# Where the projection and the statistics of the next tile stand in an attention unit

## The chip, the cores and the metric

The kernel runs on one core of a Trainium2 chip. The metric is the device time of the whole kernel in microseconds (us), lower is better. A core has a matmul engine (TensorE, in the profile PE, with its weight loads as PEld), a vector engine (VectorE, DVE), an engine for activation functions (ScalarE, ACT), a general one (GpSimd, POOL), and SyncE (SP), which here only issues DMAs. Each engine works through its own queue in order, and they meet through semaphores.

## What is computed

One layer of a transformer, for x of 8 sequences with 512 tokens of 256 values, in float32: a modulated layer norm, causal attention with 16 heads of 16 values and rotary positions, a gated residual, a second modulated layer norm, and a feed-forward layer with eight experts, of which each token takes one. Cut to what matters:

```python
h = layernorm(x) * (1 + ca) + sa
Q, K, V = h @ Wq.T + bq, h @ Wk.T + bk, h @ Wv.T + bv      # 16 heads of 16
Q, K = rope(Q, pos), rope(K, pos)
scores = where(causal, Q @ K^T / 4, -1e9)
attn = softmax(scores) @ V
x = x + ga * (attn @ Wo.T + bo)
h = layernorm(x) * (1 + cb) + sb
x = x + gb * route_prob_max * expert_of_token(h)            # 8 experts, gelu
```

The change is in the attention part alone, and there in the first three lines of it: the statistics of the layer norm, and the projection to Q and K.

## The kernel before

Tokens are cut into 32 tiles of 128 (four to a sequence), heads into four groups of four. The attention part works in 32 **units** (U = 0 to 31): unit U is one group of heads of one sequence, all 512 queries against all 512 keys. Each engine has its own loop over the units, in an order that is written out by hand: TensorE's at L791, ScalarE's at L954, VectorE's at L1192, GpSimd's at L513, SyncE's at L364.

A unit has six **shots**, s = 0 to 5. In each shot TensorE makes two things:

- the maxima products of the *next* unit V = U + 1 (`max_scores`, L646 and L653): scores in one layout, 768, 768, 1024, 1024, 1024 and 512 columns wide in the six shots, into the two banks `ps_max`. VectorE reduces them to row maxima (`maxima`, L1116). `ps_max` is a single buffer: the products of shot s wait until VectorE has reduced shot s - 1.
- the scores of *this* unit (`scores`, L680) into the two banks `ps_sc`, which ScalarE turns into exponentials (`exps`, L926). `ps_sc` is a single buffer too, and shot s waits for the exponentials of shot s - 1.

Between them the rest of the work is laid in by hand:

- the weighting of the values by the exponentials (`weigh`, L693), of which two parts of unit U - 1 stand in shot 0;
- the work on the tile T = U + 5, five ahead. `project_qk` (L599 to L607) projects its 128 tokens to 256 values of Q and 256 of K in the bank `ps_b`: a bias matmul (L604), then one float32 matmul of 512 columns for each of the KC = 2 halves of the 256 inputs (L605); each such matmul has two records in the profile. VectorE's `rope` (L1087, L1093) reads `ps_b`, GpSimd's `rotate` (L425) adds the two products, ScalarE (L890) and VectorE (`lo_parts`, L1102, L1103) split the sum into 16-bit parts, and TensorE transposes these in shot 5;
- the statistics of tile T + 1 on VectorE (`statistics`, L1063, L1065, L1067), GpSimd's power of its variance (`rstd_of`, L417), VectorE's `normalise` (L1072) in shot 4, TensorE's transposes of it (L596) at the end of the unit, and VectorE's `modulate` (L1079), whose result the next `project_qk` multiplies;
- the output projection and the residual of older units, and, once in four units (U = 11, 15, 19, 23, 27), the logits of the router for four tiles (`logit_products`, L739).

At the end of the unit VectorE negates the maxima (`negated`, L1123), TensorE transposes them with the queries (`shift_rows`, L663), and ScalarE keeps these (L919) for the next unit's scores. VectorE's `rope` follows `maxima(V, 1)`, and its `statistics` follow `maxima(V, 2)`.

Tiles 0 to 4 are projected before the units, in a lead phase, where both halves and the values' projection (L613) follow each other with nothing between. Units from 27 on have no tile to project; units from 26 on have no statistics to take. The experts' part comes behind the attention part, from about 530 us on.

Of the kernel before, what the change touches and what calls it, by code (L numbers as in the profile page):

```python
# [19 lines left out]
NT = B * QT  # L20
KC = D // P
# [45 lines left out]
def ge(eng, sem, count):  # L67

    if isinstance(count, int) and count <= 0:
        return  # L70
    eng.wait_ge(sem, count)
# [43 lines left out]
def attention_part(nc, sem, x, wq, bq, wk, bk, wv, bv, wo, bo, c, wmod, rope_cos, rope_sin, switch_w, switch_b,  # L115
                   w1, w2, row_dram, mods_dram, w_dram, logits, ident, sw_b):
    with ExitStack() as ctx:
# [3 lines left out]
        def bank(name):  # L121
            return ctx.enter_context(nc.psum_tensor(name, [P, 512], F32))
# [54 lines left out]
        ps_a, ps_b = bank("ps_a"), bank("ps_b")  # L177
# [369 lines left out]
        def _(pe):  # L547
# [51 lines left out]
            def project_qk(T, k, ps, kept_before):  # L599

                if k == 0:
                    pe.wait_ge(ht_done, KC * T + KC)
                    ge(pe, qt_kept, kept_before)
                    mm(ps, ones3[:, :], bias3[:, 0:2 * D], start=True, stop=False)  # L604
                last = mm(ps, h_t[:, k, :], w_qkv[:, k, 0:2 * D], start=False, stop=(k == KC - 1))  # L605
                if k == KC - 1:
                    last.then_inc(qk_ps, 1)  # L607
# [77 lines left out]
            def weigh(U, kb):  # L685
                par, g = place(U)
                pe.wait_ge(masked, QT * U + kb + 1)
                L = S - P * kb
                p_kb = prob[:, U % 2, P_AT[kb]:P_AT[kb + 1]].rearrange("p (j m q) -> p j m q", j=2, m=2)
                for m in range(2):  # L690
                    for j in range(2):
                        col = 2 * m + j
                        last = mm(ps_pv[32 * col:32 * col + 32, kb * P:S], v_sb[:, par, kb, HG * g + col, :],  # L693
                                  p_kb[:, j, m, :], start=(kb == 0), stop=(kb == QT - 1), skip_group_check=True)
                if kb == 0:
                    last.then_inc(pv0_ps, 1)
                if kb == QT - 1:
                    last.then_inc(pv_ps, 1)
# [92 lines left out]
            for U in range(NU):  # L791
                T, V, X, Z = U + LEAD, U + 1, U - QT, U - LAG
                for s in range(NSHOT):
                    if V < NU:
                        max_scores(V, s)
                    scores(U, s)
                    if s == 0 and U:
                        weigh(U - 1, 2)
                        weigh(U - 1, 3)
                    if s == 1 and Z > 0 and Z % QT == 0:  # L800
                        pe.wait_ge(x1_done, X)
                        logit_products(Z // QT - 1, ps_nd)
                    if s < KC and T < NT:
                        project_qk(T, s, ps_b[:, :], T)
                    if s == 1 and Z > 0 and Z % QT == 0:
                        logit_transposes(Z // QT - 1, ps_nd)
                    if Z >= 0 and s == h_shot(Z):
                        ge(pe, logits_kept, Z // QT)
                        pe.wait_ge(x1_done, X)
                        h_transposes(Z, ps_nd)  # L810
                    if s == 2:
                        if T < NT:
                            project_v(T, ps_a[:, :], T)
                        ge(pe, htr_kept, Z + 1)
                        if U:
                            tokens_first(U - 1)
                    if s == 3:
                        if U == 0:
                            pe.wait_ge(mods_kept, 1)
                        weigh(U, 0)  # L820
                    if s == 4:
                        if X >= 0:
                            pe.wait_ge(att_done, U)
                            ge(pe, x1_done, X)
                            att_transposes(X, ps_nd)
                        weigh(U, 1)
                    if s == 5:
                        if X >= 0:
                            project_out(X, ps_nd)
                        if T < NT:  # L830
                            q_transposes(T, ps_b[:, :])
                        if V < NU:
                            shift_rows(V)
                        if T < NT:
                            k_transposes(T, ps_a[:, :])
                        if T + 1 < NT:
                            if U == 0:
                                pe.wait_ge(gates_kept, 1)
                            x_transposes(T + 1, ps_nd, U)
# [171 lines left out]
        def _(dve):  # L1011
# [48 lines left out]
            def statistics(T):  # L1060
                par, t = place(T)
                dve.wait_ge(xs_loaded[loaded_by(T)], tile_loads(T))
                nc.vector.bn_stats(bn[:, :], xs[:, par, t, :]).then_inc(stats_done, 1)  # L1063
                dve.wait_ge(stats_done, T + 1)
                nc.vector.bn_aggr(mean_var[:, :], bn[:, :]).then_inc(mv_done, 1)  # L1065
                dve.wait_ge(mv_done, T + 1)
                nc.vector.tensor_scalar(var_eps[:, :], mean_var[:, 1:2], LN_EPS, None, ALU.add).then_inc(var_done, 1)  # L1067
# [68 lines left out]
            def residual(X, ps):  # L1136
                par, t = place(X)
                dve.wait_ge(xr_loaded[loaded_by(X)], tile_loads(X))
                dve.wait_ge(const_added, X + 1)
                dve.wait_ge(o_ps, X + 1)  # L1140
                x1 = rows[:, par, t, D:2 * D]
                nc.vector.tensor_tensor(x1, ps[:, KC * P:KC * P + D], x1, ALU.add).then_inc(x1_done, 1)
# [49 lines left out]
            for U in range(NU):  # L1192
                T, V, X = U + LEAD, U + 1, U - QT
                for s in range(NSHOT):
                    if V < NU:
                        maxima(V, s)
                    if s == 0 and X > 0:
                        residual(X - 1, ps_nd)
                    if s == 1 and T < NT:
                        rope(T, ps_b[:, :])  # L1200
                    if s == 2 and T + 1 < NT:
                        statistics(T + 1)
                    if s == 3 and U:
                        divide(U - 1)
                    if s == 4:
                        if T < NT:
                            lo_parts(T)
                        if T + 1 < NT:
                            normalise(T + 1)
                if V < NU:  # L1210
                    negated(V)
                if T < NT:
                    keep_qt(T, ps_b[:, :])
                if X > 0:
                    row_statistics(X - 1)
                if T + 1 < NT:
                    modulate(T + 1, ps_nd)
# [509 lines left out]
```

## Time and profile before

| | us |
|---|---|
| median of 3 runs | 790.11 |
| lowest and highest | 788.54, 791.86 |
| the profiled execution's own time | 788.82 |
| span of its instructions | 787.0 |
| busy in it: PE, DVE, ACT, POOL | 698.1, 597.4, 506.4, 455.0 |
| mean granted clock of PE | 0.967 of full |

The profile shows one execution. A row of a timeline gives the start of an instruction and its length in us, the engine, the line of the kernel, what it writes and reads, and how many neighbouring instructions are merged in the row; in brackets stands for how long the engine was idle before it, and which instruction of another engine ended that. Matmuls are pipelined, and their ends are modelled, so that one can begin before the one before it has ended; the distance from start to start is the safer measure. "PEclk" is the clock that TensorE was granted, as a part of full speed, or in tenths of it.

### The profile page before, as it was taken

The numbers are of one execution on the slowest core, as the hardware profiler recorded it, in microseconds if no ns is written. First come the engines' busy times: TensorE is split into PE (matmuls) and PEld (weight loads), VectorE is DVE, ScalarE is ACT, GpSimd is POOL, SyncE is SP. The second block draws the span as 40 slices with busy tenths as digits, with TensorE's granted clock in tenths as the row PEclk, the third lists the DMA queues.
The fourth block names the chain that finished last, engine by engine and source line by source line (L and its number), as shares of the span: only waits on it lengthen the run. The fifth ranks groups of instructions, "written<-read, shape, count | busy, mean of one in ns | idle before, by whom it ended". The sixth has DMA issues, their size and how long they took to land. (4 is left out here: it accounts for less than half of the span.)

```text
span 787.0 us, 20856 instructions
## 1 busy us (share of the span) xinstructions
PE 698.1 (89%) x7310; PEld 433.4 (55%) x7310; DVE 597.4 (76%) x1238; ACT 506.4 (64%) x1001; POOL 455.0 (58%) x577
## 2 busy tenths in 40 slices
PE   6858889999999999999999888755999999999993
PEld 4533434455455544554554443434788878788772
DVE  5767787988988978879889767348577777777774
ACT  1426788888888888888888878733444444444441
POOL 4313454777777777777777868851254444445331
PEclk8998999999999999999999999966999999999998
DMA  8104233244344443534633537539666642232100
GB/s 266 41 1 102 89 92 110 69 128 132 115 149 122 137 133 110 148 121 95 152 104 113 154 101 163 133 109 384 223 205 213 212 139 78 82 89 85 35 20 0
DMA packets 61362, 97.48 MB, mean 124 GB/s; under 512 B 8404, under 2 KB 42317, under 8 KB 60752
## 3 DMA queue, kind: packets, MB, share of 16 engines
q1 hardware_dynamic: 56272, 79.36, 34.0%
q0 software_dynamic: 4992, 16.79, 6.8%
q8 instruction: 64, 1.05, 0.5%
q14 instruction: 34, 0.28, 0.1%
HBM read 69.47 MB, written 34.51 MB: 132 GB/s over the span
## 5 line engine op out<-in xcount | busy, mean ns | idle before, releaser
L1116 DVE TENSOR_REDUCE row_max<-ps_max 128x2 f32<-128x768 f32 (+2 forms) x192 | 199.6, 1040 | 51.2 <-PE ps_max L653 51.1
L926 ACT ACTIVATE prob<-ps_sc 128x1024 f32<-128x1024 f32 (+1 forms) x192 | 169.2, 882 | 60.4 <-PE ps_sc L680 59.4
L1464 PE MATMUL ps_h<-tok_t,w_all 128*128 128x128 f16 x1872 | 156.4, 219 | 0.6 <-DVE tok_t L1639 0.3
L1464 PEld LDWEIGHTS ps_h<-tok_t,w_all 128*128 x1872 | 130.8, 98 | 41.8 <-issue 2.1
L1534 ACT ACTIVATE hid<-ps_h,b_t 128x128 f32<-128x128 f32 x312 | 89.3, 368 | 95.3 <-PE ps_h L1464 95.3
L434 POOL TENSOR_SCALAR_AFFINE_SELECT prob<-prob 128x512 f32<-128x512 f32 x128 | 82.5, 645 | 86.5 <-ACT prob L926 86.1
L1381 POOL DMA_INDIRECT slot_mem<-row_dram,token x39 | 55.7, 1428 | 120.3 <-DVE y L1674 99.8
L1477 PE MATMUL ps_y<-w_all,hid_parts 128*128 x312 | 118.0, 379 | 1.3 <-DVE hid_parts L1649 1.3
L693 PE MATMUL ps_pv<-prob,v_sb 128*32 128x512 f32 (+3 forms) x1024 | 88.8, 442 | 0.3 <-POOL prob L434 0.2
L646 PE MATMUL ps_max<-k_t,q_t 64*128 64x512 f16 (+3 forms) x512 | 68.6, 304 | 22.8 <-DVE row_max L1116 22.1
L1479 PE MATMUL ps_y<-w_all,hid_parts 128*128 x312 | 85.1, 273 | 0.0
L646 PEld LDWEIGHTS ps_max<-k_t,q_t 64*128 64x128 f16 x512 | 20.3, 93 | 117.2 <-DVE row_max L1116 64.6
L482 POOL TENSOR_TENSOR halves<-raw,halves 128x512 f16<-128x512 f32 x64 | 74.3, 1161 | 17.0 <-ACT raw L936 17.0
L680 PE MATMUL ps_sc<-q_t,k_t 64*128 64x256 f16 (+3 forms) x512 | 67.4, 300 | 5.2 <-ACT q_t L919 4.8
L1647 DVE CAST hid_parts<-hid 128x512 f16<-128x512 f32 x78 | 33.8, 433 | 48.3 <-ACT hid L1534 48.3
L605 PE MATMUL ps_b<-w_qkv,h_t 128*128 128x512 f32 x120 | 70.3, 674 | 0.0
L1398 POOL DMA_INDIRECT out<-y,token x39 | 43.0, 1104 | 29.7 <-DVE y L1674 19.6
L425 POOL TENSOR_TENSOR rot<-rot_a,rot_b 128x512 f32<-128x512 f32 x32 | 40.7, 1271 | 29.2 <-DVE rot_b L1093 28.7
L1649 DVE TENSOR_TENSOR hid_parts<-hid,hid_parts 128x512 f16<-128x512 f32 x78 | 54.2, 694 | 2.7
L653 PE MATMUL ps_max<-tri,tri_w 64*128 64x64 bf16 (+1 forms) x768 | 46.5, 199 | 0.0
L919 ACT ACTIVATE q_t<-ps_sc 128x512 f16<-128x512 f16 x64 | 34.7, 593 | 17.9 <-PE ps_sc L663 17.4
L653 PEld LDWEIGHTS ps_max<-tri,tri_w 64*128 64x128 bf16 x768 | 36.9, 95 | 12.4 <-issue 0.3
(257 smaller groups left out, 1322.3 us busy)
## 6 DMA issues: line engine op xcount, KB each, us to landing
raw<-w SPq DMA_DIRECT2D x64, 256.0 KB, 3.0
w_dram<-halves SPq DMA_DIRECT2D x64, 256.0 KB, 3.3
w_all<-w_dram SPq DMA_DIRECT2D x20, 512.0 KB, 4.6
row_dram<-rows SPq DMA_DIRECT2D x32, 256.0 KB, 3.4
w_all<-w_dram SPq DMA_DIRECT2D x3, 2048.0 KB, 13.0
mod_rows<-mods_dram SPq DMA_DIRECT2D x16, 256.0 KB, 7.2
row_dram<-mods_dram SPq DMA_DIRECT2D x32, 128.0 KB, 4.4
xs<-x SPq DMA_DIRECT2D x24, 128.0 KB, 3.3
```

What stands on the lines that cost most here:

```text
L434: nc.gpsimd.affine_select(out=diag, in_=diag, compare_op=ALU.is_ge, fill=0.0, base=0, pattern=[[0, HG], [1, P]], channel_multiplier=-1).th ...
L482: nc.gpsimd.tensor_tensor(lo, piece_raw(m)[0], hi, ALU.subtract).then_inc(w_lo[m % 2], 1)
L605: last = mm(ps, h_t[:, k, :], w_qkv[:, k, 0:2 * D], start=False, stop=(k == KC - 1))
L646: mm(ps_max[:, j, m * L:(m + 1) * L], q_t[rows, par, pair, qt * P:(qt + 1) * P], k_t[rows, par, pair, 0:L], start=(m == 0), stop=False, sk ...
L653: last = mm(o, tri_w[rows, side, :], tri[rows, 0:n, :], start=False, stop=(side == 1), skip_group_check=True)
L693: last = mm(ps_pv[32 * col:32 * col + 32, kb * P:S], v_sb[:, par, kb, HG * g + col, :], p_kb[:, j, m, :], start=(kb == 0), stop=(kb == QT ...
L926: nc.scalar.activation(p_kb[:, :, first * L:(first + n) * L], ps_sc[:, :, 0:n * L], ACT.Exp, scale=SCALE).then_inc(exp_done, 1)
L1116: nc.vector.tensor_reduce(dst, ps_max[:, :, 0:n * L].rearrange("p j (m l) -> p j m l", m=n), AX.X, ALU.max).then_inc(max_done, 1)
L1464: last = mm(o, w[:, :, k, f, :][:, bass.ds(e, 1), :].rearrange("p e m -> p (e m)"), tok_t[:, j % 2, piece, k, :], start=(n == 0 and f % HF ...
L1477: mm(ps_y[j % 2][:, :], hid_hi[:, j % 2, f, :], w2_both[:, :, f, :, :][:, bass.ds(e, 1), :, :].rearrange("p e a d -> p (e a d)"), start=(f ...
L1479: last = mm(ps_y[j % 2][:, 0:D], hid_lo[:, j % 2, f, :], w2_both[:, :, f, 0, :][:, bass.ds(e, 1), :].rearrange("p e d -> p (e d)"), start= ...
L1534: ins = nc.scalar.activation(hid[:, j % 2, f, :], ps_h[j % 2][q][:, (f % HF) * P:(f % HF + 1) * P], ACT.Gelu_apprx_tanh, bias=b1_t[:, bass ...
```

## The change

In each unit TensorE gives up the first half of the projection of queries and keys in shot 0 (bias matmul and one float32 matmul, behind the weighting), and makes bias matmul and both halves together in shot 1, behind the second maxima products and the second scores. In VectorE's queue the three instructions of the statistics move from behind the third maxima (shot 2) to between the second maxima (shot 1) and the rope. Nothing is added or removed, and what is computed stays the same.

```diff
@@ TensorE, in the loop over the units @@
                     if s == 1 and Z > 0 and Z % QT == 0:
                         pe.wait_ge(x1_done, X)
                         logit_products(Z // QT - 1, ps_nd)
-                    if s < KC and T < NT:
-                        project_qk(T, s, ps_b[:, :], T)
+                    if s == 1 and T < NT:
+                        for k in range(KC):
+                            project_qk(T, k, ps_b[:, :], T)
                     if s == 1 and Z > 0 and Z % QT == 0:
                         logit_transposes(Z // QT - 1, ps_nd)
@@ VectorE, in the loop over the units @@
                         maxima(V, s)
                     if s == 0 and X > 0:
                         residual(X - 1, ps_nd)
+                    if s == 1 and T + 1 < NT:
+                        statistics(T + 1)
                     if s == 1 and T < NT:
                         rope(T, ps_b[:, :])
-                    if s == 2 and T + 1 < NT:
-                        statistics(T + 1)
                     if s == 3 and U:
                         divide(U - 1)
```

## Rows read from the trace of the kernel before

**Rows 1.** The page, sections 1 and 2: busy time, and the clock in 40 slices.
```profile
PE 698.1 (89%) x7310; PEld 433.4 (55%) x7310; DVE 597.4 (76%) x1238; ACT 506.4 (64%) x1001; POOL 455.0 (58%) x577
...
PEclk8998999999999999999999999966999999999998
```

**Rows 2.** The waits: who waited for whom, us in all, times, the longest.
```profile
DVE rot_a L1087 <- PE ps_b L605: 16.8, 30, 3.2
```

**Rows 3.** Timeline of VectorE, a steady unit: start, length, engine, line, output and input.
```profile
309.49 0.69 DVE L1087 TENSOR_TENSOR rot_a<-ps_b,cos_t 128x512 f32<-128x512 f32 x1 [0.31 <-PE ps_b L605]
...
310.76 1.21 DVE L1116 TENSOR_REDUCE row_max<-ps_max 128x4 f32<-128x1024 f32 x1
311.89 0.42 DVE L1063 BATCH_NORM_STATS2 bn<-xs 128x6 f32<-128x256 f32 x1
...
312.56 0.15 DVE L1067 TENSOR_SCALAR var_eps<-mean_var 128x1 f32<-128x1 f32 x1
312.63 1.22 DVE L1116 TENSOR_REDUCE row_max<-ps_max 128x2 f32<-128x1024 f32 x1
...
317.68 0.20 DVE L1123 TENSOR_SCALAR q_aug<-row_max 128x16 f16<-128x16 f32 x1
...
323.70 0.69 DVE L1087 TENSOR_TENSOR rot_a<-ps_b,cos_t 128x512 f32<-128x512 f32 x1 [0.31 <-PE ps_b L605]
```

**Rows 4.** Timeline of TensorE, the same unit and the one after.
```profile
306.42 0.38 PE L604 MATMUL ps_b<-bias,ones 3*128 3x512 bf16 x1
306.73 1.13 PE L605 MATMUL ps_b<-w_qkv,h_t 128*128 128x512 f32 x2
307.79 0.34 PE L646 MATMUL ps_max<-k_t,q_t 64*128 64x384 f16 x2
...
308.02 0.38 PE L680 MATMUL ps_sc<-q_t,k_t 64*128 64x512 f16 x2
308.33 1.13 PE L605 MATMUL ps_b<-w_qkv,h_t 128*128 128x512 f32 x2
309.29 0.38 PE L731 MATMUL ps_nd<-ident,rows 128*128 128x128 f32 x2
...
317.94 0.62 PE L663 MATMUL ps_sc<-ident,q_aug 128*128 128x128 f16 x8 [0.25 <-DVE q_aug L1123]
```

**Rows 5.** Timeline, the first shot of that unit on VectorE and ScalarE.
```profile
305.71 0.95 DVE L1116 TENSOR_REDUCE row_max<-ps_max 128x2 f32<-128x768 f32 x1
305.74 1.02 ACT L926 ACTIVATE prob<-ps_sc 128x1024 f32<-128x1024 f32 x1 [0.49 <-PE ps_sc L680]
```

**Rows 6.** Timelines, products that wait for a reduction, and reductions that wait for products.
```profile
69.75 1.22 DVE L1116 TENSOR_REDUCE row_max<-ps_max 128x2 f32<-128x1024 f32 x1
...
71.51 1.23 DVE L1116 TENSOR_REDUCE row_max<-ps_max 128x2 f32<-128x1024 f32 x1 [0.55 <-PE ps_max L653]
...
312.03 0.39 PE L646 MATMUL ps_max<-k_t,q_t 64*128 64x512 f16 x2 [0.26 <-DVE row_max L1116]
...
312.32 0.33 PE L680 MATMUL ps_sc<-q_t,k_t 64*128 64x384 f16 x2
```

**Rows 7.** Timeline of TensorE in the lead phase, a projection in one piece.
```profile
28.89 1.98 PE L605 MATMUL ps_b<-w_qkv,h_t 128*128 128x512 f32 x4
30.71 1.03 PE L613 MATMUL ps_a<-w_qkv,h_t 128*128 128x256 f32 x4
```

**Rows 8.** Timeline, the first two shots of unit 0.
```profile
62.62 0.94 DVE L1116 TENSOR_REDUCE row_max<-ps_max 128x2 f32<-128x768 f32 x1
...
63.63 0.50 PE L646 MATMUL ps_max<-k_t,q_t 64*128 64x384 f16 x2
...
64.59 1.98 PE L605 MATMUL ps_b<-w_qkv,h_t 128*128 128x512 f32 x2
...
66.61 0.69 DVE L1087 TENSOR_TENSOR rot_a<-ps_b,cos_t 128x512 f32<-128x512 f32 x1 [1.38 <-PE ps_b L605]
```

**Rows 9.** Stretches: busy PE, PEld, DVE, ACT, POOL, then PEclk, DMA share, GB/s.
```profile
66.00:67.00 1.00, 1.00 (x11) 0.36 (x10) 0.39 (x1) 0.00 (x0) 0.45 (x1) 0.82 0.36 87
```

## The prediction

> **What bounds the kernel now.** I read the page first for the shares of the engines [rows 1]: TensorE is busy for 89% of the span and its clock is granted in full in nearly every slice of the attention part. High shares of two engines say little about which wait ends last, so I went on to the list of waits [rows 2]: VectorE's first rope product waited 30 times for the projection of queries and keys, 16.8 us in all. Then I laid the timelines of VectorE and TensorE of one steady unit beside each other, and followed them round.
>
> From the rope at 309.49 to the end of the negated maxima at 317.68 + 0.20 = 317.88, VectorE has no gap [rows 3]. The shift transposes of TensorE start at 317.94, right behind it [rows 4], and from there TensorE has no gap until the last pass of the next projection; the rope of the next unit starts at 323.70, 14.21 us after the last one [rows 3]. So the loop has two legs: a VectorE leg of 8.4 us, from rope to negated maxima, and a TensorE leg of 5.8 us, from shift transposes to the end of the projection. Both edits lie on it. The projection closes the TensorE leg; the statistics stand in the VectorE leg. 27 units project (units 0 to 26), 26 take statistics (0 to 25). Whatever one edit adds to a steady unit is paid some 26 times.
>
> **First part: both halves of the projection behind the second scores.** Before, the stretch in question is this [rows 4]: bias matmul at 306.42, first half at 306.73 (0.31 later), second maxima products at 307.79 (1.06), second scores at 308.02 (0.23), second half at 308.33 (0.31), and the rope at 309.49 (1.16) [rows 3]. Together 3.07 us from the bias matmul to the rope.
>
> The first half now fills a time in which TensorE would have to wait: both maxima banks form one buffer, and the second maxima products may start only when VectorE has reduced the first. That reduction runs from 305.71 to 306.66 [rows 5]. With the half gone from there, TensorE is through with the weighting at 306.42 and waits at the second maxima products; queued behind that wait are the second scores, the whole projection and the transposes of h. The hand-over from reduction to products takes 0.06 us elsewhere (311.97 to 312.03) [rows 3, 6], so the products start at 306.72. The scores follow 0.29 later, as they do behind another such wait (312.03 to 312.32) [rows 6]; they also need the first exponentials, which end at 305.74 + 1.02 = 306.76 [rows 5], before 307.01, so that doesn't bind. The bias matmul follows 0.31 behind the scores (as 308.02 to 308.33), the first half 0.31 behind the bias [rows 4].
>
> For the fused projection the lead phase has the very sequence. There the four records of a projection take 1.98 us, and the next instruction starts 1.82 us after the first [rows 7]. Split, the two pairs are followed by their next instruction after 1.06 and, where that is again a float32 operation, 0.96 (308.33 to 309.29) [rows 4]: 2.02. Fusing saves 0.20 us of TensorE, at one change from 16-bit to float32 work and back. The rope starts 0.03 behind the last record (308.33 + 1.13 to 309.49), so 2.01 from the first half to the rope.
>
> New stretch from the end of the reduction at 306.66: 0.06 + 0.29 + 0.31 + 0.31 + 2.01 = 2.98 us, against 309.49 - 306.66 = 2.83 before. **The rope comes 0.15 us later** in each of units 1 to 26: +3.9 us. The lower end takes the bias matmul 0.23 behind the scores instead of 0.31 (nearest row: 307.79 to 308.02), +0.07 per unit. The upper end denies the saving: 1.06 + 1.16 instead of 2.01, +0.36 per unit.
>
> The Trainium skill, page "TensorE: Matmul & The Clock Gate", section "Back-to-back issue gap", gives an isolated matmul's spacing as its columns over 2.4 GHz plus 2.5 ns, with no term for what its neighbours are. Worked out from it as an estimate, a half costs the same wherever it stands, and fusing saves nothing; the rows of the lead phase speak against that [rows 4, 7]. It is the second rival's side, whose price I take from rows.
>
> Four units (11, 15, 19, 23) have logit products, float32, ahead of the projection. There the bias matmul stands between two float32 pieces and adds one more change of type, 0.10 by half of the 0.20 above: +0.4 us in all, ends 0 and 0.8.
>
> **Unit 0** has no weighting, and its first maxima on VectorE end only at 62.62 + 0.94 = 63.56; the products start at 63.63 [rows 8]. Bias and first half stood wholly under that wait. Now they follow it. TensorE is at half its clock there (1.2 GHz), until about 66.36, by a granted mean of 0.82 in the microsecond from 66 [rows 9]. From products to rope takes 0.29 + 0.31 + 0.31 + 2.01 = 2.92 us at full clock. The 2.73 us up to 66.36 do half of that length's work, 1.37; the remaining 1.55 put the rope at 67.91, against 66.61 [rows 8]: +1.3 us. If the clock stays low throughout, 63.63 + 5.84 = 69.47: +2.9 us. TensorE will stand idle for some 2.4 us before, where it was busy, which makes a later rise possible. I take +1.5, nearer the lower end, because TensorE is busy without a gap from 63.63 on in either order.
>
> The Trainium skill, same page, section "What's actually happening", says that the throttled state is the default and activity lifts it; by that the idle time could only delay the rise, which is the +2.9 end.
>
> **Second part: statistics ahead of the rope.** Three VectorE instructions, 311.89 to 312.56 + 0.15 = 312.71, 0.82 us, leave the gapless leg [rows 3]. But little of it comes back. The third maxima's reduction ends at 310.76 + 1.21 = 311.97, and the fourth starts at 312.63, 0.66 later [rows 3]. Without anything between them VectorE would wait for the refill of the bank: in unit 0, where nothing is done between the fourth and fifth maxima, the distance is 71.51 - (69.75 + 1.22) = 0.54, with a wait for the products noted [rows 6]. **The gain is 0.66 - 0.54 = 0.12 us** per unit, 26 times: -3.1 us. Ends: 0 (the 0.66 stays) and 0.82 (all of it, if the refill were hidden).
>
> In their new place the statistics are covered. The second reduction starts about 0.60 behind its products (as 312.03 to 312.63) [rows 3, 6], at 307.32 at the latest, takes 0.96 and ends at 308.28; the statistics end at 309.10, and the rope is due at 309.64. Cover of 0.54 us; if it were gone, each microsecond of delay would be one of the path. Their wait for the tile of x costs nothing: it is loaded seven units ahead by the loop of SyncE. GpSimd's power of the variance still stands behind the rotation, which waits for the rope; it only finds its input earlier. No DMA moves. ScalarE gets the second scores earlier, but keys and the weighted sum are copied in its queue ahead of them.
>
> **The sum**: 3.9 - 3.1 + 1.5 + 0.4 = +2.7 us. The profiled execution has a span of 787.0 us in 788.82 us; it would become 791.5. The median of three runs is 790.11, 1.3 above the profiled one; on it I predict **792.8 us**.
>
> **The rivals.** A measurement of this kernel can't tell less than about 0.5%, 4.0 us, from no change.
>
> (A) *Forecast*: a wait takes the place of the filler, mostly repaid by fusing and by the statistics. Its own range is 790 to 796. Chance 0.60.
>
> (B) *Slower, no saving from fusing*: in the unit, weights or the change of type cost as much as before, 26 x 0.21 = 5.5 us more, 798.3 us. Place: from bias matmul to rope. It decides the sign once a steady unit is over (4.0 - 1.9) / 26 = 0.08 us longer than 14.21. For it: split passes are slower [rows 4]. Against: four passes in a row are measured at 1.98 [rows 7]. Chance 0.15.
>
> (C) *Slower, no gain from the statistics*: the refill takes 0.66 whatever stands there. 3.9 + 1.5 + 0.4 = +5.8, 795.9 us. Against: 0.54 in unit 0 [rows 6]. Chance 0.08.
>
> (D) *Small gain, the first wait is not felt*: the second products start at 306.42 and the rope keeps its place or comes earlier; then -3.1 + 1.5 = -1.6, 788.5 us. Against: one maxima buffer, and VectorE's reduction held until 306.66 by its own queue [rows 5]. Chance 0.13.
>
> (E) *The edit does what it seems to say*: the leg of VectorE gets 0.82 shorter. 26 x (0.15 - 0.82) + 1.9 = -15.5, 774.6 us. Against: the refill of 0.54 [rows 6]. Chance 0.04.
>
> **How the numbers follow.** The likeliest case gives 792.8. The range 788 to 798 takes in A, C and D and stops just short of B; outside lie B's upper half, E and a tail of A, some 2 in 10. Faster by over 0.5%: E, and 0.03 of D with unit 0 at its cheap end: 0.07. Slower by over 0.5%: B 0.15, C 0.05, and 0.08 of A, where unit 0 costs 2.9 and a unit some 0.1: 0.28. Within: 0.65.
>
> **What would show it.** Rope to rope in steady units: 14.24 says A, 14.45 B, 14.36 C, 14.09 D, 13.5 E. The idle time before the second maxima products should appear as a new wait of TensorE for VectorE's first reduction, about 0.3 us, some 26 times; the wait of the rope in the list should change little in place but shrink or grow with what the statistics fill. Four float32 passes within 1.98 us confirm the saving. Third to fourth reduction: 0.54 instead of 0.66. Rope of unit 0: at about 68. The prediction is wrong at its root if the loop is no longer closed by TensorE's projection, or if the clock falls inside the attention units.

## The result, and the profile of the changed kernel

The changed kernel takes 793.33 us (median of 13 runs, 791.60 to 796.87), the kernel before, in as many runs beside it, 789.72. The ratio is 1.0041, with a 95% interval from 1.0022 to 1.0060: some 3 us slower, 0.4%. The prediction was 792.8 us, within 788 to 798. The profiled execution has a span of 792.5 us in 794.36 us. (The kernel before ran again beside each later run; its medians there are 789.83 to 790.87 us, and each ratio below is to the executions beside it.)

Page of the changed kernel, sections 1 and 2, and two rows of its list of waits; they answer to [rows 1, 2].

```profile
PE 700.2 (88%) x7310; PEld 439.3 (55%) x7310; DVE 598.8 (76%) x1238; ACT 503.5 (64%) x1001; POOL 455.6 (57%) x577
...
PEclk8997999999999999999999989966799999999997
```
```profile
DVE rot_a L1088 <- PE ps_b L605: 30.9, 30, 3.6
...
PE ps_max L646 <- DVE row_max L1117: 29.2, 92, 2.3
```

The shares tell nothing. The waits do: TensorE waits for VectorE's reductions 92 times, 29.2 us (66 times, 22.1 us before), the wait that was forecast. The rope's own wait for the projection was to change little and grew from 16.8 to 30.9 us. That is no loss: VectorE is through with the work ahead of the rope sooner, and stands idle for 0.74 us where it was 0.31. Timeline of VectorE in a steady unit, to be read beside [rows 3]:

```profile
311.65 0.69 DVE L1088 TENSOR_TENSOR rot_a<-ps_b,cos_t 128x512 f32<-128x512 f32 x1 [0.74 <-PE ps_b L605]
...
312.92 1.21 DVE L1117 TENSOR_REDUCE row_max<-ps_max 128x4 f32<-128x1024 f32 x1
314.68 1.23 DVE L1117 TENSOR_REDUCE row_max<-ps_max 128x2 f32<-128x1024 f32 x1 [0.55 <-PE ps_max L653]
...
317.93 0.42 DVE L1104 TENSOR_TENSOR k_aug<-rot,k_aug 128x256 f16<-128x256 f32 x1
318.26 0.72 DVE L1073 TENSOR_SCALAR xhat<-xs,mean_var,rstd 128x256 f32<-128x256 f32 x1
...
319.62 0.21 DVE L1124 TENSOR_SCALAR q_aug<-row_max 128x16 f16<-128x16 f32 x1
...
325.74 0.69 DVE L1088 TENSOR_TENSOR rot_a<-ps_b,cos_t 128x512 f32<-128x512 f32 x1 [0.75 <-PE ps_b L605]
```

From rope to rope it is now **14.09 us, not 14.21**: the steady unit has become faster. The legs, parted here at the start of the negated maxima (the prediction's 8.4 and 5.8 are parted at their end), are 319.62 - 311.65 = 7.97 on VectorE (8.19 before) and 325.74 - 319.62 = 6.12 on TensorE (6.02 before). Timelines of TensorE, first the end of the first reduction on VectorE, to be read beside [rows 4, 5]:

```profile
307.77 0.94 DVE L1117 TENSOR_REDUCE row_max<-ps_max 128x2 f32<-128x768 f32 x1
308.77 0.34 PE L646 MATMUL ps_max<-k_t,q_t 64*128 64x384 f16 x2 [0.24 <-DVE row_max L1117]
...
309.00 0.38 PE L680 MATMUL ps_sc<-q_t,k_t 64*128 64x512 f16 x2
...
309.31 0.39 PE L604 MATMUL ps_b<-bias,ones 3*128 3x512 bf16 x1
...
309.63 1.98 PE L605 MATMUL ps_b<-w_qkv,h_t 128*128 128x512 f32 x4
```

The reduction ends at 308.71; products after 0.06, scores after 0.23, bias after 0.31, projection after 0.32, rope after 2.02: 2.94 us, where 2.98 was forecast and 2.83 was the time before. The loss is elsewhere: above all in unit 0, to be read beside [rows 8, 9].

```profile
63.71 0.50 PE L646 MATMUL ps_max<-k_t,q_t 64*128 64x384 f16 x2 [2.33 <-DVE row_max L1117]
...
65.21 3.78 PE L605 MATMUL ps_b<-w_qkv,h_t 128*128 128x512 f32 x4
...
69.03 0.69 DVE L1088 TENSOR_TENSOR rot_a<-ps_b,cos_t 128x512 f32<-128x512 f32 x1 [2.98 <-PE ps_b L605]
```
```profile
66.00:69.00 3.00, 3.00 (x6) 0.75 (x6) 0.05 (x1) 0.00 (x0) 0.53 (x1) 0.50 0.35 87
...
455.00:460.00 5.00, 4.44 (x26) 1.54 (x22) 3.00 (x4) 3.04 (x5) 1.50 (x4) 0.51 0.00 1
```

Four records take 3.78 us, at half the clock throughout, and the rope comes at 69.03. The second window shows another stretch at 1.2 GHz, from 455 to 462 us, inside the attention units, among those that no longer project.

The table has, for every kernel of this study, the time from the last rope of the lead phase to the rope of unit 0; the part of it from the start of unit 0's first reduction on; a steady unit; and the time from that last lead rope to the rope of unit 26, all from one trace each; then the medians. The time to unit 26 ends before the later clock changes. But the time to unit 0 holds one that isn't the order's: in "statistics only", "halves apart" and "every fourth unit old" TensorE was at half its clock for 6.8 us shortly behind the last lead rope (from 46.5, 47.1 and 47.7 us on), and the first reduction of unit 0 came 22.34 to 22.65 us behind that rope instead of 20.10; in "unit 0 old, warm" for 3.4 us (from 46.4), and it came after 21.10. The column "from its first reduction" leaves that out.

| kernel | to unit 0 | from its first reduction | steady unit | to unit 26 | median us | ratio to before, 95% interval |
|---|---|---|---|---|---|---|
| before | 24.09 | 3.99 | 14.21 | 396.09 | 789.72 | |
| changed | 26.42 | 6.32 | 14.09 | 398.04 | 793.33 | 1.0041 (1.0022 to 1.0060) |
| projection only | 26.43 | 6.32 | 14.31 | 402.39 | 798.70 | 1.0088 (1.0055 to 1.0121) |
| statistics only | 25.99 | 3.49 | 14.33 | 400.73 | 795.38 | 1.0051 (1.0029 to 1.0073) |
| unit 0 as before | 23.95 | 3.85 | 14.09 | 395.62 | 790.37 | 1.0003 (0.9981 to 1.0025) |
| halves apart | 28.67 | 6.33 | 14.40 | 408.24 | 800.78 | 1.0118 (1.0086 to 1.0149) |
| filled wait | 23.98 | 3.87 | 14.09 | 395.54 | 792.47 | 1.0019 (0.9997 to 1.0042) |
| late mask | 24.06 | 3.95 | 14.24 | 396.73 | 793.40 | 1.0031 (1.0011 to 1.0051) |
| more statistics | 26.76 | 6.31 | 14.09 | 398.33 | 794.49 | 1.0051 (1.0026 to 1.0075) |
| every fourth unit old | 26.11 | 3.46 | 14.09, 14.26, 14.31 | 397.82 | 791.91 | 1.0009 (0.9985 to 1.0034) |
| later mask | 24.47 | 4.09 | 14.09 | 394.09 | 790.07 | 0.9990 (0.9974 to 1.0005) |
| before, warm | 24.17 | 4.07 | 14.21 | 396.52 | 789.80 | 0.9994 (0.9977 to 1.0010) |
| unit 0 old, warm | 25.18 | 4.08 | 14.09 | 396.81 | 789.07 | 0.9979 (0.9963 to 0.9994) |
| combined | 22.80 | 2.70 | 14.09 | 392.39 | 786.54 | 0.9950 (0.9930 to 0.9970) |

### The profile page after: what moved, and what is told of

It reads as the page before. It is cut to its first block and busy times, and to the rows that moved or that the text cites. A ratio compares the mean times of both kernels' runs of the same rounds, so it can differ in the third digit from the quotient of the medians.

```text
span 792.5 us, 20856 instructions
## 1 busy us (share of the span) xinstructions
PE 700.2 (88%) x7310; PEld 439.3 (55%) x7310; DVE 598.8 (76%) x1238; ACT 503.5 (64%) x1001; POOL 455.6 (57%) x577
## 5 line engine op out<-in xcount | busy, mean ns | idle before, releaser
L434 POOL TENSOR_SCALAR_AFFINE_SELECT prob<-prob 128x512 f32<-128x512 f32 x128 | 86.9, 679 | 91.3 <-ACT prob L927 88.6
L646 PE MATMUL ps_max<-k_t,q_t 64*128 64x512 f16 (+3 forms) x512 | 69.2, 307 | 29.9 <-DVE row_max L1117 29.2
L605 PE MATMUL ps_b<-w_qkv,h_t 128*128 128x512 f32 x120 | 63.1, 650 | 0.0
```

Source lines behind the costliest of these rows:

```text
L434: nc.gpsimd.affine_select(out=diag, in_=diag, compare_op=ALU.is_ge, fill=0.0, base=0, pattern=[[0, HG], [1, P]], channel_multiplier=-1).th ...
L646: mm(ps_max[:, j, m * L:(m + 1) * L], q_t[rows, par, pair, qt * P:(qt + 1) * P], k_t[rows, par, pair, 0:L], start=(m == 0), stop=False, sk ...
```

## The experiments

**The two parts apart.** The first run leaves the statistics in shot 2:

```diff
-                    if s < KC and T < NT:
-                        project_qk(T, s, ps_b[:, :], T)
+                    if s == 1 and T < NT:
+                        for k in range(KC):
+                            project_qk(T, k, ps_b[:, :], T)
```

> The first part of the change alone: the whole projection behind the second scores, the statistics where they were. In the steady units of the changed kernel the rope comes 2.94 us behind the end of the first reduction instead of 2.83, so this part alone should cost 0.11 us per steady unit, some 0.35 in the four units behind the logit products, and 2.3 us in unit 0. Theory (each part has its own price, and they add up): rope to rope 14.32 us in a steady unit, 795 to 797 us in all. Rival (the part costs nothing per unit and the whole loss is unit 0): 14.21, 792.5 us.

The second moves the statistics alone:

```diff
+                    if s == 1 and T + 1 < NT:
+                        statistics(T + 1)
                     if s == 1 and T < NT:
                         rope(T, ps_b[:, :])
-                    if s == 2 and T + 1 < NT:
-                        statistics(T + 1)
```

> The second part of the change alone: statistics between second maxima and rope, the projection in two halves as before. Theory: they have cover in their new place only because the fused projection starts VectorE's second reduction 1.4 us earlier. Without it the reduction ends at 309.19 in the unit shown and the rope was due at 309.49, so statistics of 0.82 us push the rope by about 0.5 us, of which 0.12 come back at the fourth reduction: 14.6 us from rope to rope, about 799 to 800 us in all. Rival (the statistics are worth their 0.12 us wherever they stand ahead of the rope): 14.09, 787 us.

Measured: 14.31 and 14.33 us. Timelines of VectorE, first of the projection alone:

```profile
315.34 0.69 DVE L1088 TENSOR_TENSOR rot_a<-ps_b,cos_t 128x512 f32<-128x512 f32 x1 [1.48 <-PE ps_b L605]
...
321.71 0.85 DVE L1104 TENSOR_TENSOR k_aug<-rot,k_aug 128x256 f16<-128x256 f32 x1
...
323.53 0.21 DVE L1124 TENSOR_SCALAR q_aug<-row_max 128x16 f16<-128x16 f32 x1
...
329.65 0.69 DVE L1088 TENSOR_TENSOR rot_a<-ps_b,cos_t 128x512 f32<-128x512 f32 x1 [1.48 <-PE ps_b L605]
```

and of the statistics alone:

```profile
312.46 0.41 DVE L1063 BATCH_NORM_STATS2 bn<-xs 128x6 f32<-128x256 f32 x1
...
313.12 0.15 DVE L1067 TENSOR_SCALAR var_eps<-mean_var 128x1 f32<-128x1 f32 x1
313.20 0.68 DVE L1087 TENSOR_TENSOR rot_a<-ps_b,cos_t 128x512 f32<-128x512 f32 x1
...
321.15 0.21 DVE L1123 TENSOR_SCALAR q_aug<-row_max 128x16 f16<-128x16 f32 x1
```

The projection alone lengthens TensorE's leg to 6.12 and leaves VectorE's at 8.19; VectorE then idles 1.48 us ahead of the rope. The statistics alone shorten VectorE's leg to 7.95, but the rope (the next one starts at 327.53) stands behind them without a gap, so the other leg grows to 327.53 - 321.15 = 6.38. That is +0.36, where 0.5 was expected, and VectorE's leg lost 0.24, where 0.12 was expected: 14.33 instead of 14.6. The size of my expectation was off, its sign right. **Each part alone costs, 0.88% and 0.51%, and together they cost no more than either.** The traces say it more sharply than the medians. From the rope of unit 0 to that of unit 26, the projection alone costs 3.96 us and the statistics alone 2.74; together they win 0.38 (375.96, 374.74 and 371.62 against 372.00). Up to unit 26, with unit 0 in it, it is +6.3, +4.6 and +1.95; but of the +4.6, 2.4 are the low clock behind the lead phase that the table names, which the place of the statistics doesn't explain. The idle time that one part opens is the room that the other needs.

**Unit 0.**

```diff
-                    if s == 1 and T < NT:
+                    if s < KC and T < NT and U == 0:
+                        project_qk(T, s, ps_b[:, :], T)
+                    if s == 1 and T < NT and U:
                         for k in range(KC):
                             project_qk(T, k, ps_b[:, :], T)
```

> The changed kernel, but in unit 0 the first half of the projection stays in the first shot, as before. Theory: unit 0 costs 2.3 us by itself, since there the half stood wholly under a wait and TensorE is at half its clock; so the rope of unit 0 is back at 66.6 and the kernel at about 791.0, 0.2% above the kernel before. Rival (the loss is spread over the other units, or a slower clock later in the run costs it): less than 1 us is won, 792.5 or more.

Measured: 23.95 us to unit 0, units at 14.09, 790.37 us, ratio 1.0003. With one unit of 27 in the old order the measurable loss is gone. Up to unit 26 the trace is 2.4 us shorter (395.62 against 398.04), the medians 3.0; the rival's "less than 1 us" fits neither.

```diff
+                    if s == 0 and U == 0:
+                        ge(pe, qt_kept, T)
+                        for _ in range(20):
+                            mm(ps_b[:, 0:P], ident16[:, :], ident16[:, :], start=True, stop=True)
```

> The changed kernel with 20 small matmuls without use laid into the wait of unit 0 (into the bank of the projection, whose first real product overwrites them), so that TensorE is busy there. The order of the real work stays that of the changed kernel. Theory: of the 2.4 us that unit 0 costs, about 1.3 are the order itself, and about 1.1 the clock, which rises some 3 us later because TensorE stood idle for 2.3 us; with the wait filled, last lead rope to rope of unit 0 takes 25.4 us instead of 26.4, and the kernel about 792.2. Rival (the clock rises late for another reason, such as where the execution happens to stand): 26.4 us stays.

Measured: 23.98 us, not 25.4. Timeline of TensorE and VectorE, and the stretches with the granted clock (the last number but two):

```profile
60.71 1.84 PE L800 MATMUL ps_b<-ident 128*128 128x128 f16 x20
...
63.91 1.98 PE L605 MATMUL ps_b<-w_qkv,h_t 128*128 128x512 f32 x4
...
65.93 0.69 DVE L1092 TENSOR_TENSOR rot_a<-ps_b,cos_t 128x512 f32<-128x512 f32 x1 [0.74 <-PE ps_b L605]
```
```profile
60.00:62.00 2.00, 1.83 (x16) 1.40 (x17) 1.90 (x4) 1.14 (x2) 0.00 (x0) 0.53 0.00 0
62.00:64.00 2.00, 1.49 (x20) 0.79 (x17) 1.51 (x3) 0.29 (x1) 0.00 (x0) 1.00 0.16 20
```

The clock was back at 2.4 GHz at 62, four microseconds sooner than even in the kernel before, and the whole projection ran at full speed. The median doesn't show this gain: the profiled execution is the fastest of ten (787.80 us), and their median, 792.47, is what was expected with 25.4. So the trace gives the price of the clock where the filling works; how often it works is not shown. That the clock follows the order, and not where the execution happens to stand, is seen in all traces together: with nothing filled in, the low stretch at unit 0 lasts 6.8 us in the six kernels that keep its old order, and 10.2 us in the four that have the new one. The split into 1.3 for the order and 1.1 for the clock was taken from the wrong reference: the kernel before pays for a low clock itself. What the order costs at an equal clock came from the next pair.

```diff
                 if s == 3:
                     raw_part(ps_nd, 1, 2).then_inc(gates_ps, 1)
+                    ge(pe, qt_kept, LEAD)
+                if s >= 3:
+                    for _ in range((6, 18, 12)[s - 3]):
+                        mm(ps_b[:, 0:P], ident16[:, :], ident16[:, :], start=True, stop=True)
             shift_rows(0)
```

> The kernel before with 36 small matmuls without use in the waits of the last three maxima shots ahead of unit 0, so that TensorE doesn't fall to 1.2 GHz there. Theory: the kernel before pays for the low clock in unit 0 too, and the changed order costs 1.2 us more than the old one at an equal clock: with full clock, last lead rope to rope of unit 0 takes 22.8 us instead of 24.1 (changed order with its wait filled: 24.0), the kernel 1.3 us less, 788.8. Rival (the clock isn't what unit 0 waits for): 24.1 us, 790.1.

> The changed kernel with unit 0 in the old order and the same 36 matmuls ahead of unit 0. If all prices are right and add up: unit 0 at 22.8 us, steady units 14.09, which is 1.3 + 0.4 us less than the kernel before, 788.4 us, ratio about 0.998, 5 us less than the changed kernel. Rival (as in the run of four units in a row, what is won in one place is given back in the next): 790 us or more.

Neither reached 22.8: 24.17 and 25.18 us, of which the second has 1.0 from the low clock behind the lead phase. The small matmuls kept the clock up ahead of unit 0, until 62.7 and 63.5, and then it fell, in the 1.3 us for which TensorE still waited in unit 0. As tests of the price they are inconclusive. The changed kernel with unit 0 in the old order and the 36 matmuls is nevertheless 0.2% faster than the kernel before (ratio 0.9979, 0.9963 to 0.9994).

**Is fusing worth 0.2 us?** Here the second scores part the two halves:

```diff
                         max_scores(V, s)
+                    if s == 1 and T < NT:
+                        project_qk(T, 0, ps_b[:, :], T)
                     scores(U, s)
...
                     if s == 1 and T < NT:
-                        for k in range(KC):
-                            project_qk(T, k, ps_b[:, :], T)
+                        project_qk(T, 1, ps_b[:, :], T)
```

> The changed kernel with the two halves of the projection parted by the second scores: second maxima products, bias and first half, scores, second half. The same work behind the same wait; only the four float32 records no longer stand in one piece. Theory (fusing saves a change between 16-bit and float32 work each way): the rope comes 0.2 us later, 14.30 us from rope to rope in a steady unit, 798 to 799 us in all. Rival (the spacing of the records doesn't depend on their neighbours): 14.09, 793.3 us.

```profile
316.20 0.34 PE L646 MATMUL ps_max<-k_t,q_t 64*128 64x384 f16 x2 [0.23 <-DVE row_max L1118]
...
316.53 0.38 PE L604 MATMUL ps_b<-bias,ones 3*128 3x512 bf16 x1
...
316.84 1.12 PE L605 MATMUL ps_b<-w_qkv,h_t 128*128 128x512 f32 x2
...
317.90 0.39 PE L680 MATMUL ps_sc<-q_t,k_t 64*128 64x512 f16 x2
...
318.22 1.13 PE L605 MATMUL ps_b<-w_qkv,h_t 128*128 128x512 f32 x2
...
319.39 0.69 DVE L1089 TENSOR_TENSOR rot_a<-ps_b,cos_t 128x512 f32<-128x512 f32 x1 [1.05 <-PE ps_b L605]
```

From the products on: 0.33, 0.31, 1.06, 0.32, 1.17. The two halves take 2.23 us instead of 2.02, the 0.21 that was forecast. Another 0.10 comes from the scores, which no longer start 0.23 behind the products. The unit takes 14.40 us, 0.31 more than fused, where I expected 0.21 more. The saving is real; without its 0.21 the steady unit would take 14.30 us, more than the 14.21 before. That it comes from the change between 16-bit and float32 work is argued: no run changes the type alone.

**The cover of the statistics.**

```diff
                 nc.vector.bn_stats(bn[:, :], xs[:, par, t, :]).then_inc(stats_done, 1)
+                if T > LEAD:
+                    nc.vector.bn_stats(bn2[:, T % 2, :], xs[:, par, t, :])
+                    nc.vector.bn_stats(bn3[:, T % 2, :], xs[:, par, t, :])
```

> The changed kernel with two further statistics instructions of 0.42 us, without use, behind the first one of each tile from the sixth on. VectorE is idle for 0.74 us between statistics and rope in a steady unit. Theory: 0.74 of the added 0.90 us are covered, 0.16 are paid: 14.25 us from rope to rope, about +4 us in all, 797 us. Rival (what stands ahead of the rope is on the path in full): 15.0 us, about 817 us.

```profile
311.12 0.41 DVE L1068 BATCH_NORM_STATS2 bn<-xs 128x6 f32<-128x256 f32 x1
311.45 0.41 DVE L1069 BATCH_NORM_STATS2 bn<-xs 128x6 f32<-128x256 f32 x1
...
312.36 0.69 DVE L1093 TENSOR_TENSOR rot_a<-ps_b,cos_t 128x512 f32<-128x512 f32 x1 [0.23 <-PE ps_b L607]
```

The added instructions start 0.33 us apart, so they cost less than their length; the idle time ahead of the rope shrinks from 0.74 to 0.23, by 0.51, and the unit keeps its 14.09 us. What was added was smaller than meant, so that nothing had to be paid; that it is covered in full speaks for the theory, and the rival is out.

**Where 0.11 us came from that nobody had forecast.** In the changed kernel VectorE's k part takes 0.42 us, where it took 0.85 in the kernel before and in the run with the projection alone. GpSimd's third mask starts beside it. Timelines of GpSimd and VectorE in the kernel before:

```profile
315.79 0.65 POOL L434 TENSOR_SCALAR_AFFINE_SELECT prob<-prob 128x512 f32<-128x512 f32 x1 [0.46 <-ACT prob L926]
315.87 0.85 DVE L1103 TENSOR_TENSOR k_aug<-rot,k_aug 128x256 f16<-128x256 f32 x1
...
316.64 0.40 DVE L1072 TENSOR_SCALAR xhat<-xs,mean_var,rstd 128x256 f32<-128x256 f32 x1
```

and of GpSimd in the changed kernel, to be read beside VectorE's rows of the result:

```profile
317.95 0.89 POOL L434 TENSOR_SCALAR_AFFINE_SELECT prob<-prob 128x512 f32<-128x512 f32 x1 [0.46 <-ACT prob L927]
```

The k part is 0.43 us shorter, but the `normalise` behind it now takes 0.72 us instead of 0.40, so that 0.11 are left. Two runs delay that mask in the kernel before, first by 16 cleared values per row, then by 256:

```diff
                 low_piece(2 * U)
+                pool.wait_ge(exp_done, NSHOT * U + EXP_UPTO[2])
+                nc.gpsimd.memset(late[:, :], 0.0).then_inc(late_done, 1)
                 clear_future(U, 2)
```

> The kernel before, with one change of its own: GpSimd clears 16 unused values (0.17 us) ahead of the third mask of each unit, behind that mask's wait. Theory: the unforeseen 0.12 us per unit of the changed kernel come from the order in which VectorE's k part (0.85 us before, 0.42 in the changed kernel) and GpSimd's mask reach a resource that they share; if the mask starts after the k part instead of 0.08 us before it, the k part takes 0.42 us here too and the unit 14.10 us, about 787.5 us in all. Rival (the 0.12 us belong to the place of the statistics or of the projection): 14.21 us stays, 790 us.

> The run with the late mask again, since the cleared values took 0.11 us only and the mask still started 0.03 us ahead of VectorE's k part (316.66 against 316.69, the k part 0.88 us long). Now 256 float32 values per row are cleared, so that the mask comes after the k part has started. Theory (the k part takes 0.85 instead of 0.42 us where a mask of GpSimd started first, and the order of the two is what the changed kernel happens to turn round): k part 0.42 us, VectorE's leg of a unit 8.08 instead of 8.19 us, rope to rope 14.10. Rival (the k part is slow here for another reason): 14.21 to 14.24 us again.

Timelines of GpSimd and VectorE, first with the short delay:

```profile
316.66 0.64 POOL L436 TENSOR_SCALAR_AFFINE_SELECT prob<-prob 128x512 f32<-128x512 f32 x1
316.69 0.88 DVE L1107 TENSOR_TENSOR k_aug<-rot,k_aug 128x256 f16<-128x256 f32 x1
```

then with the longer one:

```profile
315.53 0.31 POOL L529 MEMSET late<- 128x256 f32 x1 [0.45 <-ACT prob L930]
315.62 0.42 DVE L1107 TENSOR_TENSOR k_aug<-rot,k_aug 128x256 f16<-128x256 f32 x1
315.80 1.48 POOL L436 TENSOR_SCALAR_AFFINE_SELECT prob<-prob 128x512 f32<-128x512 f32 x2
```

The first delay was too short: the mask still came 0.03 us ahead, and nothing was won (14.24 us). The median of that run is 0.31% above the kernel before; its loop is only 0.6 us longer, and the rest is open. With the second the k part takes 0.42 us and the unit 14.09, in the old order of TensorE and VectorE. Up to unit 26 that is 2.0 us less, which the whole kernel's ratio can't tell from nothing (0.9990, 0.9974 to 1.0005). So the gain belongs to the order in which two engines reach a shared resource, and the change turned that order round. By the traces this is how: with the statistics gone, TensorE's fourth and fifth shots stand closer (1.78 us from scores to scores, 1.87 before), ScalarE's exponentials follow the scores after 0.61 instead of 0.51 us, as it is still busy with the parts of the tile, and the mask that waits for them keeps its place, 6.30 us behind the rope, while the k part comes after 6.28 us instead of 6.38: 0.02 us ahead of the mask instead of 0.08 behind it. The Trainium skill, page "SBUF — State Buffer", section "SBUF: two separate sides", calls the port pair that VectorE and GpSimd share an exclusive lock: whichever of the two starts first holds it for its whole instruction. A VectorE instruction with two inputs in SBUF needs it only against a GpSimd instruction that reads SBUF. The trace agrees: the k part has two such inputs and takes longer behind the mask, by 0.43 us, a little less than the 0.57 us that were left of the mask; and it runs in 0.42 us beside the clearing, which reads nothing.

**Every fourth unit in the old order.** Behind the logit products (units 12, 16, 20 and 24, and also 8) a changed unit takes 14.51 us instead of 14.26: the first reduction ends late there, and TensorE waits 0.38 us for it. The diff is the one of unit 0 with `U % QT == 0` for both parts.

> The changed kernel with every fourth unit (0, 4, 8, ...) in the old order, both parts. These are unit 0 and the units behind the logit products, where the first reduction ends late (0.38 us of wait instead of 0.24). Theory: the old order takes 14.26 us there instead of 14.51, and 24.0 instead of 26.4 in unit 0; the others keep 14.09. Sum of 2.3 + 5 x 0.25 = 3.6 us less than the changed kernel, 789.5 us, some 0.1 to 0.3% faster than the kernel before. Rival (the gain of a unit depends on what its neighbours do, since the next one inherits its lateness): the fourth units' gain is given back, 790.5 us or more.

```profile
65.75 0.94 DVE L1119 TENSOR_REDUCE row_max<-ps_max 128x2 f32<-128x768 f32 x1
...
69.21 0.69 DVE L1090 TENSOR_TENSOR rot_a<-ps_b,cos_t 128x512 f32<-128x512 f32 x1 [0.63 <-PE ps_b L605]
...
240.29 0.69 DVE L1090 TENSOR_TENSOR rot_a<-ps_b,cos_t 128x512 f32<-128x512 f32 x1 [0.31 <-PE ps_b L605]
...
254.60 0.69 DVE L1090 TENSOR_TENSOR rot_a<-ps_b,cos_t 128x512 f32<-128x512 f32 x1 [0.75 <-PE ps_b L605]
```

The fourth units take 14.26, as expected, but the unit after each takes 14.31 instead of 14.10, as the last two ropes show. The rival holds: of the 0.25 us won, 0.21 are given back. The legs explain it. VectorE's long leg of an old unit (8.19) is followed by the longer TensorE leg of a new one (6.12): 14.31. Unit 0 did gain: from the start of its first reduction to its rope it takes 69.21 - 65.75 = 3.46 us, where the changed kernel takes 6.32. The 26.11 us of the table come from ahead of it: TensorE was at half its clock from 47.7 to 54.5 us, where it had the full clock in the kernel before, and the first reduction started 2.5 us late.

**All that the runs point to, without the change.** The longer delay of the mask, the 36 small matmuls, and 14 more in unit 0:

```diff
                     if s < KC and T < NT:
                         project_qk(T, s, ps_b[:, :], T)
+                    if s == 0 and U == 0:
+                        ge(pe, kt_kept, LEAD)
+                        for _ in range(14):
+                            mm(ps_a[:, 0:P], ident16[:, :], ident16[:, :], start=True, stop=True)
```

> The kernel before with three things that the earlier runs point to, and neither part of the change: the later mask (14.09 us instead of 14.21 per unit), the 36 small matmuls ahead of unit 0, and 14 more behind the first half of the projection in unit 0, since with 36 alone TensorE was still idle for 1.3 us there and fell to 1.2 GHz at 63.0. Theory: units at 14.09, 2.4 us less over 26 units, and unit 0 at 22.8 us, 1.3 less: 786.8 us, ratio 0.995 to the kernel before. Rival (the clock falls in unit 0 in any case, as in both runs with the 36): the units' gain alone, 788.0, ratio 0.997.

```profile
63.67 1.13 PE L609 MATMUL ps_b<-w_qkv,h_t 128*128 128x512 f32 x2
...
64.83 0.69 DVE L1099 TENSOR_TENSOR rot_a<-ps_b,cos_t 128x512 f32<-128x512 f32 x1 [0.31 <-PE ps_b L609]
```

Unit 0 takes 22.80 us and the units 14.09, both as expected; 786.54 us, ratio 0.9950 (0.9930 to 0.9970). It is faster than both kernels. It also gives the price that the warm pair could not: at full clock the old order takes 22.80 us to unit 0, the changed one, with its wait filled, 23.98 (2.70 and 3.87 from the first reduction on), by one trace each. **The order itself costs 1.2 us in unit 0. The low clock costs 1.3 us there in the kernel before (24.09 against 22.80) and 2.4 in the changed one (26.42 against 23.98).**

## Why the prediction was right, point by point

**What bounds the loop**: right. Two legs from rope to rope add up to the unit by themselves, so the sums 8.19 + 6.02, 7.97 + 6.12, 8.19 + 6.12 and 7.95 + 6.38 (before, changed, projection alone, statistics alone) prove nothing. What speaks for it is that the projection alone moves one leg and leaves the other as it is, and that 0.51 us of added work off the legs cost a steady unit nothing. With the statistics alone the rope stands right behind VectorE's own work, and the projection no longer closes the loop.

**The wait instead of the filler**: right, +0.11 instead of +0.15. The term that was too large is that from products to scores, 0.23 instead of 0.29; the row it was taken from [rows 6] had been chosen for its wait, not for its width. The saving of fusing is 0.21 in its own experiment, forecast 0.20.

**The statistics**: right, 0.66 down to 0.55, forecast 0.54. The cover was to be 0.54 us and is 0.74, since TensorE's second maxima and with them VectorE's second reduction came sooner (309.21, 0.44 behind the start of the products) than the 0.60 that I took as a latest time.

**What was missing**: 0.11 us per unit on VectorE, from the shared resource. It makes the steady unit's sum -0.12 instead of +0.03: the forecast had its sign wrong. Case D's 14.09 us came true by a mechanism that was not D's, since the first wait is felt. I read the k part's 0.85 us as its cost; its 0.42 us in every fourth unit of the trace of before would have shown that half of it was a wait.

**Logit units**: the size right, the reason not. They take 14.76 instead of 14.78, a gain of 0.02 us where a steady unit gains 0.12; the difference is the +0.10 that was forecast for them. But the bias matmul costs nothing extra behind the logit products (these take 0.58 us to the next product in both kernels); it is the hand-over from the first reduction that takes 0.14 instead of 0.06 us there (336.90 to 337.04 in unit 19). What was missed is one unit later: +0.25 us, four times and in unit 8, and +0.10 in unit 4. The first reduction ends late there, and the first half of the projection had covered that. I had taken one unit as the pattern for all 26.

**Unit 0**: +2.33 us, forecast +1.5 between 1.3 and 2.9. The clock did stay low (rise at 69.4), the dearer end that the idle time made possible. It was the wrong choice between two ends that were both named; and that end was priced too high, 2.9 for 2.33, by doubling every term: the first half starts 1.50 us behind the products, where 1.82 was taken, and the rope 3.82 behind the half, where 4.02 was.

The sum up to the rope of unit 26 was to be +2.7 us and is 398.04 - 396.09 = +1.95: unit 0 0.8 dearer, the units 1.6 cheaper, both errors of the size of the result. They offset each other in part, so that 792.8 and 793.33 lie so close is in part luck. The forecast was "within 0.5%", 0.65 likely, and 0.4% came out; the 13 executions of each kernel tell that much from no change, which the prediction had thought too little to be told.

One of the prediction's own signs of being wrong at its root came true by its words: the clock fell inside the attention units, at 455 us. It fell behind the last projection, where it can't touch the sum that was forecast, and it belongs to what follows.

The span of the profiled execution grew by 5.5 us. Of the 3.5 beyond those 1.95, 2.0 lie between the rope of unit 26 and the last reduction (56.4 us against 54.4), where the changed kernel ran at 1.2 GHz from 455 on; a low clock near that place shows in 8 of the 14 profiled executions of this study, among them two of kernels that leave TensorE's order alone (the late and the later mask), so it isn't tied to the change. 1.4 lie behind the attention part. The two profiles overstate the difference: the mean granted clock is 0.967 in that of before, where 35 executions beside later runs have 0.964 in the mean, and 0.955 in that of the changed kernel, whose 13 have 0.9585. **Open** is the rest of the median: the loop explains +1.95 us of the 3.2 (1.7 to 4.7) that the ratio gives, which its interval allows to be all. How often each kernel meets the later clock change can't be told from one profile of each.

## What to carry to other kernels

Two edits that cost 0.9% and 0.5% alone can win a little together in the steady unit, where one opens the idle time that the other fills: price them as a pair, on the two legs of the loop, and look for the leg that the next unit inherits. The exceptional unit deserves its own sum: here one unit of 27 carried the loss (+2.33 us), and the other 26 together won 0.38, though five of them lost 0.25 each. Work under a wait can have a second use on TensorE: moved away here, the low clock lasted 10.2 us instead of 6.8. Before it is moved, see what the granted clock does there. And before a difference is put down to a place, see whether it was there already ahead of that place: 2.4 us of low clock behind the lead phase look like a cost of unit 0 in three of these traces.

## What the runs showed of the hardware

- Whether GpSimd's mask starts 0.08 us before or 0.02 us after a VectorE instruction with two inputs in SBUF decides whether that takes 0.85 or 0.42 us; turned over, the mask takes 0.89 instead of 0.65 and VectorE's next instruction 0.72 instead of 0.40, so that 0.11 are won. A delay of GpSimd by 0.31 us in each unit made the loop 2.0 us shorter.
- Four float32 records of 512 columns take 2.02 us to the next reader in one piece, and 2.23 in two pieces with 16-bit work between them (that work's own time left out): parting them costs TensorE 0.2 us.
- TensorE's clock differs in the same place between kernels that are nearly the same: in unit 0 it was granted in full from 62, 66 or 69 us on, and this is worth up to 2.4 us of the unit. Where TensorE waited through unit 0's first reduction with nothing to do, the low stretch was 10.2 us (four of four traces); where the first half of the projection stood in that wait, 6.8 (six of six). With the waits of the last maxima shots and of unit 0 filled by 50 small matmuls it stayed at 2.4 GHz there, in the one trace of that kernel.
